# A transformer block on one core: the maximum written negated, prologue reordered, and VectorE's low parts put ahead of the next chunk's steps

## The reference, cut to what matters

```python
x = x + xattn(layernorm(x), ctx, ctx, mask, Wq, bq, Wk, bk, Wv, bv)   # x (4, 1024, 256), ctx (4, 154, 256)
x = x + ffn(layernorm(x), gate_w, w_gate, w_up, w_down, sw_gate, sw_up, sw_down)

def xattn(query, key, value, mask, ...):
    q, k, v = query @ Wq + bq, key @ Wk + bk, value @ Wv + bv
    scores = where(mask, q @ k.T / sqrt(256), -inf)
    return softmax(scores) @ v

def ffn(x, ...):                       # 16 experts, hidden 128; all are computed, the best 8 weighted
    scores = sigmoid(l2norm(xf) @ l2norm(gate_w).T)
    combine = top-8 scores over their sum, 0 for the other experts
    y = (silu(xf @ w_gate[e]) * (xf @ w_up[e])) @ w_down[e]
    return sum_e combine[e] * y[e] + (silu(xf @ sw_gate) * (xf @ sw_up)) @ sw_down
```

## Time and profile before

| what | value |
|---|---|
| median of 3 runs | 650.99 us (650.79 to 651.32) |
| the profiled execution, its own time | 650.85 us |
| its span, first to last instruction | 648.7 us |
| TensorE busy | 634.6 us, 98% |
| TensorE's weight loads busy | 551.5 us, 85% |
| VectorE busy | 472.7 us, 73% |
| GpSimd busy | 294.7 us, 45% |
| ScalarE busy | 235.7 us, 36% |
| mean granted TensorE clock | 0.997 |

### The profile page before, as it was taken

One profiled execution on the slowest core, in us unless ns is written; L12 is line 12 of the kernel. 1 busy time (PEld: TensorE's weight loads), 2 busy tenths in 40 slices (PEclk: granted clock), 3 DMA queues, 4 the chain that ended last, 5 costly groups with the idle time before them and its releaser, 6 DMA issues.

```text
span 648.7 us, 10466 instructions
## 1 busy us (share of the span) xinstructions
PE 634.6 (98%) x3688; PEld 551.5 (85%) x3688; DVE 472.7 (73%) x941; ACT 235.7 (36%) x500; POOL 294.7 (45%) x275
## 2 busy tenths in 40 slices
PE   8898999999999999999999999999999999999997
PEld 7576888889888888888888898888888888888886
DVE  3779897868967588766868689675887768575443
ACT  5644444333243323433243332433234332432221
POOL 2517687333743356333563337433464334423333
PEclk9999899999999999999999999999999999999999
DMA  7265663424225324053244342263240531242100
GB/s 212 68 168 193 175 176 79 149 70 151 63 35 198 90 83 97 24 174 107 74 89 131 89 148 64 36 198 98 73 98 22 177 107 42 56 132 98 65 1 33
DMA packets 112655, 67.19 MB, mean 104 GB/s; under 512 B 80996, under 2 KB 102396, under 8 KB 112604
## 3 DMA queue, kind: packets, MB, share of 16 engines
q1 hardware_dynamic: 111516, 65.74, 36.0%
q10 hardware_dynamic: 1088, 0.79, 0.4%
HBM read 55.79 MB, written 10.42 MB: 102 GB/s over the span
## 4 chain that ended last, share of the span: by engine, by line
PE 91%; DVE 5%; issue 2%; ACT 1%; POOL 1%; POOLq 0%; ACTq 0%; DVEq 0%
PE y_ps L393 9%; PE gate_ps L395 9%; PE gate_ps L394 9%; PE up_ps L395 9%; PE up_ps L394 9%; PE gate_ps L393 9%; PE up_ps L393 9%; PE y_ps L394 9%; PE y_ps L395 9%; PE f_ps L538 2%; DVE hs L1155 1%; DVE W L999 1%; PE up_ps L402 1%; PE f_ps L575 1%; PE f_ps L393 1%
## 5 line engine op out<-in xcount | busy, mean ns | idle before, releaser
L1351 POOL TENSOR_TENSOR hidden<-hidden,cb 128x512 f32<-128x512 f32 x128 | 193.9, 1515 | 278.5 <-DVE hidden L1149 234.3
L866 ACT ACTIVATE hidden<-gate_ps 128x512 f32<-128x512 f32 x136 | 81.3, 598 | 292.9 <-PE gate_ps L395 292.9
L1145 DVE SCALAR_TENSOR_TENSOR hidden<-hidden,gate_ps 128x512 f32<-128x512 f32 x136 | 92.7, 681 | 102.9 <-ACT hidden L866 102.7
L393 PE MATMUL y_ps<-W,hs 128*128 128x256 f32 x544 | 154.7, 284 | 5.0 <-DVE hs L1155 5.0
L394 PE MATMUL y_ps<-W,hs 128*128 128x256 f32 x544 | 151.6, 279 | 0.0
L395 PE MATMUL y_ps<-W,hs 128*128 128x256 f32 x544 | 151.4, 278 | 0.0
L1155 DVE TENSOR_TENSOR hs<-hidden,hs 128x512 fp32r<-128x512 f32 x136 | 111.1, 817 | 21.8 <-ACT hs L873 21.6
L393 PEld LDWEIGHTS y_ps<-W,hs 128*128 128x128 f32 x544 | 102.2, 188 | 13.6 <-ACT hs L873 5.0
L393 PE MATMUL gate_ps<-xT,W 128*128 128x512 f32 x272 | 107.9, 397 | 0.0
L395 PE MATMUL gate_ps<-xT,W 128*128 128x512 f32 x272 | 107.6, 396 | 0.0
L394 PE MATMUL gate_ps<-xT,W 128*128 128x512 f32 x272 | 107.3, 395 | 0.0
(11 more groups left out here) (162 smaller groups left out, 664.0 us busy)
## 6 DMA issues: line engine op xcount, KB each, us to landing
cb<-c_rows SPq DMA_DIRECT2D x64, 512.0 KB, 4.8
blocks<-in_x_dram SPq DMA_DIRECT2D x28, 128.0 KB, 2.9
xin<-in_x_dram SPq DMA_DIRECT2D x7, 512.0 KB, 4.1
t_rows<-blocks SPq DMA_DIRECT2D x28, 128.0 KB, 2.7
xs<-t_rows SPq DMA_DIRECT2D x7, 512.0 KB, 3.5
out_dram<-x SPq DMA_DIRECT2D x7, 512.0 KB, 6.2
p_rows<-blocks SPq DMA_DIRECT2D x28, 80.0 KB, 2.3
stage<-in_L_ffn_w_gate_dram SPq DMA_DIRECT2D x16, 128.0 KB, 2.5
```

What stands on the lines that cost most here:

```text
L393: mm(ps, lh, rh, start=first and i == 0, stop=False)
L866: af(ew[:, i, :], gate_ps[:, i, :], ACT.Tanh, scale=0.5).then_inc(tanh_done, 1)
L1145: V_.scalar_tensor_tensor(out=ew[:, i, :], in0=ew[:, i, :], scalar=1.0, in1=gate_ps[:, i, :], op0=ALU.add, op1=ALU.mult).then_inc(silu_don ...
L1351: pg.tensor_tensor(h[:, i, :], ew[:, i, :], cb[:, pair % PLACES, (e - 1) % 2, :], ALU.mult) \
```

## The change

Five things are changed.

1. `mask_and_max` writes the maximum negated (`negate=True`), straight into `nmax`; the instruction of line 1070 goes, with the semaphore `maxes`. GpSimd's `add_bias` waits for `scaled` in its place.
2. Other steps in the tables: `exps(1)` from 2 to 2.5, `tanh_scores` from 13 to 13.5 (ScalarE); `swap_p` from 2.5 to 3 (VectorE); `add_bias` from 9.5 to 12.5 (GpSimd).
3. In every step of every chunk, VectorE does `hidden_lo(s+1)` (and in chunk 0 `split_lo`) ahead of `front(s)` and `soon(s)`. `swap_p`, now at 3, thus stands behind `silu_up(5)` and `hidden_lo(4)`, where it stood ahead of both. In chunk 0 ScalarE does `hidden_hi(s+1)` ahead of `split_hi(s+5)`.
4. Another order in the prologue on TensorE, ScalarE and VectorE. The values' tails get a semaphore of their own (`vt0_split`).
5. In the last chunk TensorE does `gate` and `up` of expert 16 ahead of `down(13)`, not behind it.

```diff
-ACT_AT = dict(exps=(1.5, 2), probs_hi=(5,), t2_hi=(11.5,), read_z=(12.5,), tanh_scores=(13,), combine_rows=(15,))
-DVE_AT = dict(maxes=(.5, 1.5), swap_p=(2.5,), sum_reciprocal=(3.5,), probs_lo=(5,), residual=(6, 6.5),
+ACT_AT = dict(exps=(1.5, 2.5), probs_hi=(5,), t2_hi=(11.5,), read_z=(12.5,), tanh_scores=(13.5,), combine_rows=(15,))
+DVE_AT = dict(maxes=(.5, 1.5), swap_p=(3,), sum_reciprocal=(3.5,), probs_lo=(5,), residual=(6, 6.5),
...
-POOL_SOON = dict(add_bias=(9.5,), ln1_std=(11.5, 11.5), add_bv=(13.5, 14.5))
+POOL_SOON = dict(add_bias=(12.5,), ln1_std=(11.5, 11.5), add_bv=(13.5, 14.5))
...
@@ TensorE, prologue
             attend(0, 0)
-            turn_router()
             attend(0, 1)
             values(1, y_ps[:, 0, 0:D])
+            turn_router()
@@ TensorE, steps
                 for s in range(NE):
+                    if not ahead and s + AHEAD == NE - 1:
+
+                        gate(c, NE - 1)
+                        up(c, NE - 1)
                     down(c, s)
                     if ahead:
                         front(s, c + 1)
-                    if (s + AHEAD < NE or ahead) and not (c == 0 and s == 1):
+                    if (s + AHEAD < NE - 1 or ahead) and not (c == 0 and s == 1):
                         gate(c, s + AHEAD)
                         up(c, s + AHEAD)
@@ ScalarE, prologue
             exps(0, 0)
-            write_vt_hi()
+            exps(0, 1)
+            vt_hi_first()
             write_v_hi(0, y_ps[:, 0, 0:D])
-            exps(0, 1)
             probs_hi_first(0)
             probs_hi_first(1)
+            write_vt_hi()
...
             router_hi()
-            split_hi(3)
             t2_hi_first(0)
             t2_hi_first(1)
+            split_hi(3)
@@ ScalarE, steps
+                    if s + 1 < NE or ahead:
+                        hidden_hi(c, s + 1)
                     if c == 0 and s + EARLY < NE:
                         split_hi(s + EARLY)
-                    if s + 1 < NE or ahead:
-                        hidden_hi(c, s + 1)
@@ VectorE, mask_and_max
-                V_.tensor_reduce(rsum[:, 2 * q:2 * q + 2], att[:, 2 * q:2 * q + 2, 0:KEYS], AX_X, ALU.max) \
-                    .then_inc(maxes, 1)
-                dve.wait_ge(maxes, upto(c, 2, q + 1))
-                V_.tensor_scalar(nmax[:, 2 * q:2 * q + 2], rsum[:, 2 * q:2 * q + 2], -1.0, None, ALU.mult) \
+                V_.tensor_reduce(nmax[:, 2 * q:2 * q + 2], att[:, 2 * q:2 * q + 2, 0:KEYS], AX_X, ALU.max, negate=True) \
                     .then_inc(maxed, 1)
@@ VectorE, prologue
-            router_scaled()
-            write_vt_lo()
+            vt_lo_first()
             write_v_lo(0, y_ps[:, 0, 0:D])
             sum_reciprocal(0)
             probs_lo_first(0)
             probs_lo_first(1)
+            write_vt_lo()
+            router_scaled()
             residual(0, 0)
             ln2(0, 0)
             residual(0, 1)
+            ln2(0, 1)
             ln2_scale(0, 0)
-            ln2(0, 1)
             ln2_scale(0, 1)
@@ VectorE, steps
+                    if s + 1 < NE or ahead:
+                        hidden_lo(c, s + 1)
+                    if c == 0 and s + EARLY < NE and s + EARLY not in POOL_SPLITS:
+                        split_lo(s + EARLY)
                     if ahead:
                         front(s, c + 1)
                     if c + 2 < CHUNKS:
                         soon(s, c + 2)
-                    if c == 0 and s + EARLY < NE and s + EARLY not in POOL_SPLITS:
-                        split_lo(s + EARLY)
-                    if s + 1 < NE or ahead:
-                        hidden_lo(c, s + 1)
                     if ahead:
                         front(s + .5, c + 1)
@@ GpSimd, add_bias
-                pool.wait_ge(maxes, upto(c - 1, 2, 2))
+                pool.wait_ge(scaled, upto(c - 1, 2, 2))
```

More of the change, by code:

```diff
@@ L166, in xattn_moe_kernel @@
         (consts_set, tail_zeroed, ctx_turned, ctxT_read, wq_turned, wq_summed, wq_mean, wqT_read, kt_made, kt_read, a_made, a_read,
-         bq_spread, brow_made, brow_scaled, v_made, v_hi, v_lo, vt_made, vt_split, vt_loaded, gate_summed, gate_inv, gate_scaled,
+         bq_spread, brow_made, brow_scaled, v_made, v_hi, v_lo, vt_made, vt0_split, vt_split, vt_loaded, gate_summed, gate_inv, gate_scaled,
          gate_turned, gate_split, keep_set, pads_set, bias_first, w_hi, w_lo_dve, w_lo_pool) = (
@@ L170, in xattn_moe_kernel @@
                              "kt_read", "a_made", "a_read", "bq_spread", "brow_made", "brow_scaled", "v_made",
-                             "v_hi", "v_lo", "vt_made", "vt_split", "vt_loaded", "gate_summed", "gate_inv", "gate_scaled", "gate_turned",
+                             "v_hi", "v_lo", "vt_made", "vt0_split", "vt_split", "vt_loaded", "gate_summed", "gate_inv", "gate_scaled", "gate_turned",
                              "gate_split", "keep_set", "pads_set", "bias_first", "w_hi", "w_lo_dve", "w_lo_pool"))
-        (ln1_stats, ln1_rstd, x_swapped, p_swapped, x2_swapped, t1_turned, t1_read, bias_added, x_biased, scored, scaled, maxes, maxed, exped,
+        (ln1_stats, ln1_rstd, x_swapped, p_swapped, x2_swapped, t1_turned, t1_read, bias_added, x_biased, scored, scaled, maxed, exped,
          rsummed, p_turned, p_hi, p_lo, attended, x2_made, ln2_stats, ln2_rstd, inv_norms, ln2_done, t2_turned, t2_hi,
@@ L178, in xattn_moe_kernel @@
             sem(n) for n in ("ln1_stats", "ln1_rstd", "x_swapped", "p_swapped", "x2_swapped", "t1_turned", "t1_read", "bias_added", "x_biased", "scored",
-                             "scaled", "maxes", "maxed", "exped", "rsummed", "p_turned", "p_hi", "p_lo", "attended",
+                             "scaled", "maxed", "exped", "rsummed", "p_turned", "p_hi", "p_lo", "attended",
                              "x2_made", "ln2_stats", "ln2_rstd", "inv_norms", "ln2_done", "t2_turned", "t2_hi",
@@ L311, in move_v_tails @@
             def move_v_tails():
-                sp.wait_ge(vt_split, 4)
+                sp.wait_ge(vt_split, 2)
                 for row, part in ((0, HI), (PAD, HI), (2 * PAD, LO)):
@@ L489, in values @@
                     pe.wait_ge(v_lo, 1)
-                    pe.wait_ge(vt_split, 4)
+                    pe.wait_ge(vt_split, 2)
                 elif b == 2:
@@ L773, in write_v_hi, with vt_hi_first @@
                 af(V[:, b, HI, :], ps, ACT.Copy).then_inc(v_hi, 1)
-            def write_vt_hi():
+            def vt_hi_first():
                 act.wait_ge(vt_made, 1)
@@ L779, in write_vt_hi @@
                     ins = af(Vtail[row:row + PAD, 0, :], y_ps[0:PAD, 0, D:2 * D], ACT.Copy)
-                ins.then_inc(vt_split, 1)
+                ins.then_inc(vt0_split, 1)
+            def write_vt_hi():
+                act.wait_ge(v_lo, 1)
                 af(vt[:, HI, :], y_ps[:, 0, D:2 * D], ACT.Copy).then_inc(vt_split, 1)
@@ L971, in mean_wq, with vt_lo_first, write_vt_lo @@
                 V_.tensor_scalar(wq_sum[:, KD:2 * KD], wq_sum[:, 0:KD], -1.0 / D, None, ALU.mult).then_inc(wq_mean, 1)
-            def write_vt_lo():
-                dve.wait_ge(vt_split, 2)
+            def vt_lo_first():
+                dve.wait_ge(vt0_split, 1)
                 dve.wait_ge(v_hi, 1)
                 V_.tensor_tensor(Vtail[2 * PAD:STACK, 0, :], y_ps[0:PAD, 0, D:2 * D], Vtail[0:PAD, 0, :].bitcast(F32),
-                                 ALU.subtract).then_inc(vt_split, 1)
+                                 ALU.subtract).then_inc(vt0_split, 1)
+            def write_vt_lo():
+                dve.wait_ge(vt_split, 1)
                 V_.tensor_tensor(vt[:, LO, :], y_ps[:, 0, D:2 * D], vt[:, HI, :].bitcast(F32), ALU.subtract) \
@@ L1074, in sum_reciprocal @@
                 dve.wait_ge(exped, upto(c, TILES, TILES))
-                dve.wait_ge(maxed, upto(c, 2, 2))
                 V_.reciprocal(rsum, esum).then_inc(rsummed, 1)
```

## The result

The changed kernel takes 684.13 us (median of five runs, 683.56 to 687.34) against 650.99 before (650.56 to 652.28 beside it). The ratio is 1.052, with a 95% interval of 1.0495 to 1.0545: slower by 33 us, 7.6 more than forecast, and 1.1 us beyond the end of the range. The profiled execution is the longest of the five: 687.34 us of its own time, a span of 685.2 us between its first and last instruction, 36.5 more than before.

The account below looks back on a forecast made before the run. TensorE was taken as the bound. From 650.85 us: +15.6 (`attend` waits), +2.0 (chunk 1's `attend`), -2.0 (gains at `down(10)` and the tail), +10.2 (clock) = 676.7, stated as 676.5; likeliest case 671 to 683, whole range 664 to 683.

Parts of the forecast that it names:

- What bounds the kernel: TensorE alone sets the time from 97 to 640 us, without idle time; slack at chunk 1's `attend` is 0.55 us.
- The attend waits: Chunks 2 to 7: TensorE waits at each `attend` for probabilities delayed by the later `swap_p`, 6 x 2.6 = 15.6 us.
- The clock: Half-clock stretches behind six of seven new `attend` waits, each longer than 2.06 us, at 1.7 us each: +10.2 us.
- `add_bias` at 12.5: On GpSimd, the later step has slack of several microseconds and costs 0.
- rival 3: More waits per chunk, at `logits` behind `ln2_scale`, or seven clock falls with 3.1 us waits: 684.6 us; chance 0.09.
- Chunk 1's attend: The first `attend` of chunk 1 moves from 77.47 to 79.5 (75.3 to 80.7), +2.0 us.
- Down(10): In chunk 0, TensorE's 0.89 us wait ahead of `down(10)` goes, as `hidden_lo(10)` stands ahead of the front.
- The steady chunks' order: `tanh_scores` and `top_eight` changing order around `hidden_lo` costs 0.
- The tail: In the last two `down`, earlier `gate` and `up` of expert 16 remove waits of 0.92 + 0.16 = 1.1 us.
- The negated maximum: Removes 16 instructions, one of 1.58 us in the prologue; the gain is swallowed by chunk 1's `attend` wait: 0.

Follow-up runs that it names:

- run 3: The kernel before with only `swap_p` moved from step 2.5 to 3: 657.73 us, ratio 1.0076.
- run 4: The kernel before with only VectorE's new step order in all chunks and `tanh_scores` at 13.5, `swap_p` staying at 2.5: 665.99 us, ratio 1.0237.
- run 2: The changed kernel with only `add_bias` put back to step 9.5: 677.78 us, ratio 1.0366 to the kernel before.
- run 5: The changed kernel with `swap_p` back at 2.5 and `add_bias` back at 9.5: 659.14 us, ratio 1.0130 to the kernel before.
- run 7: The kernel of run 5 with VectorE's old step order in chunk 0 alone: 655.77 us, ratio 1.0075 to the kernel before.
- run 6: The kernel of run 5 with VectorE's old step order in all chunks: 652.10 us, ratio 1.0008 to the kernel before.
- run 8: The changed kernel with 18 dummy transposes on TensorE ahead of each first `attend` of chunks 2 to 7: 680.19 us, ratio 1.0410 to the kernel before.
- run 11: The kernel of run 6 with `read_a_rest(0)` and `read_z(0)` ahead of `split_hi(3)` and `split_hi(4)` in ScalarE's prologue: 649.66 us, ratio 0.9976 to the kernel before.
- run 10: The kernel of run 9 with `gate` and `up` of expert 16 ahead of `down(13)` in the last chunk: 649.10 us, ratio 0.9957 to the kernel before.
- run 9: The kernel before with only the maximum written negated, and the semaphore of `add_bias` to match: 649.75 us, ratio 0.9962.

## Why the prediction was right and wrong

**What bounds the kernel: right.** TensorE was the bound for 543 us with 0.55 us of slack at `attend`, and everything made later showed at full size.

**The attend waits: right, with mechanism and size.** Forecast 6 x 2.6 = 15.6, measured 14.3, with the slower start behind them 15.5. The way from the swap to the load took 5.75 for 5.97. The 2.0 us for one DMA from the Trainium skill, "DMA: Bandwidth & Descriptors", section "Anatomy of one DMA", which the prediction held against its rows, stand there for DMAs that GpSimd issues, while SyncE issues these; the rows were the right guide. That the swap and `hidden_lo(6)` act together was in the steps, and runs 3 and 4 show it: neither alone makes more than 0.4 us at most of these places (one wait of 1.21 in run 3).

**The clock: the price right, the rule wrong.** 1.7 us a fall is right, and by chance so is the number, six of the eight places. But that a wait is "longer than the 2.06 that was followed by a half-clock stretch" does not decide: the clock stayed behind 2.21 and 2.55, in run 2 behind five of six waits of 2.06 to 2.51, in run 5 behind 2.78, and fell behind 2.19. I had also set the fall behind `down(10)` to none, and had six of seven `attend` waits with one; it was five, and `down(10)`.

**The step that failed: `add_bias` at 12.5 "has slack of several microseconds: 0".** It costs 4.8 to 6.4 us, the largest single term that the sum had wrong. I asked when its result is needed, which is late, and not what GpSimd does to VectorE while it runs. I had used this effect for the first of the low parts and for `split_lo(10)`, so the rows were there. The Trainium skill, "GPSIMD Engine Reference", section "1. Specifications", says that GpSimd shares its SBUF interface with VectorE instructions that have two SBUF inputs; this trace agrees (3.42 against 1.29 us for `t2_lo`). In rival 3 I did have a wait at `logits`, but from `ln2_scale` behind `hidden_lo(9)`; run 2 shows that with `add_bias` back it isn't there. That rival 3's 684.6 lies so near the 684.13 measured is luck: the waits at `logits` had another cause than it names, and not all seven falls came.

**Chunk 1's attend: +3.9 for +2.0.** The part `split_lo` on GpSimd holding the second low part came as drawn (2.17 us for 0.68). The swap was later than my 63.3: two instructions ahead of it were held, the first by GpSimd's `weighted` (59.68 to 61.37), the second by its weight split (62.85 to 64.69).

```profile
60.12 2.06 DVE L1010 TENSOR_TENSOR W<-stage,W 128x768 fp32r<-128x768 f32 x1
...
63.43 1.82 DVE L1162 TENSOR_TENSOR hs<-hidden,hs 128x512 fp32r<-128x512 f32 x1
65.17 1.44 DVE L1044 STREAM_TRANSPOSE blocks<-att 128x640 f32<-128x640 f32 x1
```

My bounds, 75.3 to 80.7, took the backlog only up to 64.3. With 65.17 in place of 63.3 in the steps that gave 79.5 it is 81.4.

**Down(10): the sign was wrong.** I had the 0.89 wait go; it became 2.68, with a fall. I looked at the two things that were ahead of `hidden_lo(10)` and no longer are, and not at what the order does to expert 10's way before it. `hidden_lo(8)` is now held 2.28 us by GpSimd's `split_lo(12)`; `ln2` stands behind it, GpSimd's norm waits for `ln2`, and `weighted(9)` and then all that follows for that. Rows of this chain:

```profile
89.95 2.28 DVE L1162 TENSOR_TENSOR hs<-hidden,hs 128x512 fp32r<-128x512 f32 x1
...
95.54 0.63 ACT L880 ACTIVATE hs<-hidden 128x512 fp32r<-128x512 f32 x1 [2.91 <-POOL hidden L1359]
96.20 0.69 DVE L1162 TENSOR_TENSOR hs<-hidden,hs 128x512 fp32r<-128x512 f32 x1 [1.73 <-ACT hs L880]
...
97.81 2.35 DVE L1025 TENSOR_SCALAR xn<-x,meanvar,small 128x256 f32<-128x256 f32 x4
100.20 2.08 DVE L1049 STREAM_TRANSPOSE blocks<-xn 128x512 f32<-128x512 f32 x2
...
103.48 0.68 DVE L1162 TENSOR_TENSOR hs<-hidden,hs 128x512 fp32r<-128x512 f32 x1
```

Between `hidden_lo(9)` and `hidden_lo(10)` lie 7.3 us: `split_lo`, the front's four scales and two transposes now stand between them. Before, it was 4.7 us, with two scales and two transposes. The prediction's "stands ahead of the front" held for the front of step 9; the front of step 8 and 8.5 had moved in behind `hidden_lo(9)`.

**The steady chunks' order: 0.5 to 0.6 us a chunk, put at 0** (3.7 in all in run 7, 3.9 in run 4). VectorE is far from full, but a low part 0.1 to 0.5 us late is a wait at once.

**The gains: small but not all swallowed.** The tail gave 0.84 for 1.1. The negated maximum, put at 0 in the changed kernel, is worth 2.3 us by itself; in the changed kernel TensorE comes to chunk 1's `attend` at 74.20, 3.3 us earlier than before, and the wait up to 81.38 takes it, as the prediction said.

Against the sum: +3.9 for +2.0, +1.8 for -0.9 (2.7 off), +3.1 for 0 at the logits, -0.8 for -1.1, 10.2 for 10.2, 15.5 for 15.6; and some 3 in small waits and slow starts that the sum didn't have. Forecast +25.8, measured +36.5 in the profiled execution and +33.1 by the medians. Not settled: what besides the length of a wait makes the clock fall, and the whole reason why the same change in order costs 14 us on the kernel before (run 4) and 7 between runs 5 and 6. The traces put the difference in chunk 0: up to chunk 2's `attend` it costs 10.9 us in the one and 4.8 in the other, behind it 3.9 and 3.2. Part of it is that run 6 has the wait for `down(9)` of its own.

## What to carry to other kernels

Where the bounding engine has no idle time, every step that is moved must be checked for two things, not one: when its result is needed, and which instructions of other engines it holds while it runs. Putting the low parts ahead of the next chunk's steps cost time in every form run here, since the next chunk's work is on a long way through DRAM; whether it pays once the start of that way is moved forward was not tried. Changes that share one slack aren't additive: measure each alone and all together, and take the parts that pay. Here the negated maximum and the tail are 0.4% faster than the kernel before; with all the rest it is 5% slower.

## What the runs showed of the hardware

- **The clock's fall is not set by the wait's length alone.** In the changed kernel it fell behind idle times of 2.19, 2.24, 2.35, 2.68 and 2.80 us, and stayed at 1.00 behind 2.21 and 2.55; it stayed behind 2.12 (run 8), 2.48 (run 11), 2.78 (run 5) and five of six of 2.06 to 2.51 (run 2). Each half-clock stretch was 3.4 us long (6.8 in chunk 1, begun at 77.98 within the wait of 7.18), and cost half of its busy part. The Trainium skill, "TensorE: Matmul & The Clock Gate", section "Part 1: The HAM clock gate", has the gate keep its own time, independent of the kernel. That would let equal waits end differently, as they do here; no run here tests it.
- **VectorE held by GpSimd.** In the changed kernel a two-input instruction of 0.69 us took 1.82 or 2.28, and one of 0.68 took 2.17, beside GpSimd's weight split; two of `t2_lo` took 3.42 beside `weighted` and `add_bias`, 2.35 beside `weighted` alone, and 1.29 undisturbed. Instructions with one tensor input were held too: a sign change of 128x2 took 1.58 beside the weight split (median 0.17), and two scales of 128x256 took 2.79 beside `weighted` and `add_bias` in run 10, and 0.73 in its next chunk.
- **The sign costs nothing in the reduction**: 0.47 us without it (15.70 in the kernel before) and with it (run 9).
- **TensorE starts slowly behind a wait**: 0.17 to 0.28 us beyond the wait itself, at each `attend` of chunks 2 to 7 in the changed kernel.
